# ELU feature map of the keys: exp straight from the copied keys with a fused min-add, and the next tile's layer norm emitted two groups earlier

## The reference, cut to what matters

```python
xn = layernorm(x)                                   # over 1024 channels
# attention part ("ripple"), 8 heads of 128 channels, S = 4096
q, k, v = split(xn @ Wqkv, 3)
tele = softmax(q . k[pos - offset] / sqrt(128)) @ v[pos - offset]   # offsets 0, 1, 2, 4, ..., 4096
conv = causal depthwise convolution of v, 7 taps
fq, fk = elu(q) + 1, elu(k) + 1
low  = fq @ (fk^T v) / (fq . sum(fk) + 1e-6)
attn = xn + (tele + conv + low) @ Wo
# ffn part
xr, xk = mu_r*xn + (1-mu_r)*shift(xn), mu_k*xn + (1-mu_k)*shift(xn)
ffn = sigmoid(xr @ Wr^T) * (relu(xk @ Wk^T)^2 @ Wv^T)
y = x + attn + ffn
```

## Time and profile before

| | us |
|---|---|
| median of 2 runs | 2516.59 |
| the two runs | 2481.43 and 2551.75 |
| the profiled execution, device time | 2494.07 |
| its span, slowest core (core 0) | 2492.4 |
| spans of the 8 cores | 2428.7 to 2492.4 |
| busy on core 0: PE / DVE / ACT / POOL | 1494.7 / 1427.4 / 687.4 / 117.9 |

### The profile page before, as it was taken

One profiled execution on the slowest core, in us unless ns is written; L12 is line 12 of the kernel. 1 busy time (PEld: TensorE's weight loads), 2 busy tenths in 40 slices (PEclk: granted clock), 3 DMA queues, 4 the chain that ended last, 5 costly groups with the idle time before them and its releaser, 6 DMA issues.

```text
span 2492.4 us, 32693 instructions; the slowest of 8 cores (2428.7 to 2492.4 us)
## 1 busy us (share of the span) xinstructions
PE 1494.7 (60%) x10400; PEld 826.0 (33%) x10400; DVE 1427.4 (57%) x2064; ACT 687.4 (28%) x960; POOL 117.9 (5%) x137
## 2 busy tenths in 40 slices
PE   0078766796668765777695336455464836365474
PEld 0033323233233332433343214233251716244261
DVE  0355764745648456485475683838374654837375
ACT  0033231322322313223141213233241514133141
POOL 0001010010010100101010000000000000000000
PEclk9998877777877778877696567677686968677786
DMA  9610402203113022030222604041311204040300
GB/s 150 107 43 26 137 33 68 87 16 111 59 34 110 26 85 85 15 130 26 60 77 57 163 9 122 14 118 19 106 31 57 81 0 128 9 119 18 110 19 34
DMA packets 75230, 168.08 MB, mean 67 GB/s; under 512 B 38080, under 2 KB 38208, under 8 KB 69952
## 3 DMA queue, kind: packets, MB, share of 16 engines
q1 hardware_dynamic: 59632, 100.98, 14.0%
q0 software_dynamic: 15440, 65.02, 9.7%
HBM read 113.55 MB, written 67.11 MB: 72 GB/s over the span
## 4 chain that ended last, share of the span: by engine, by line
PE 40%; DVE 28%; DMA 13%; issue 10%; ACT 7%; DVEq 1%; SPq 0%; POOL 0%; ACTq 0%; POOLq 0%
DVE s_zb L1018 8%; PE PS L465 6%; PE PS L602 5%; PE PS L545 5%; PE PS L573 5%; DVE s_cv L280 4%; PE PS L894 3%; PE PS L1051 2%; PE PS L632 2%; PE PS L943 2%; PE PS L898 2%; PE PS L1054 2%; DMA s_vr<-vt_sp 2%; PE PS L946 2%; DMA s_p<-p_sp 2%
## 5 line engine op out<-in xcount | busy, mean ns | idle before, releaser
L465 PE MATMUL PS<-s_xnfm,s_wq 128*128 128x512 bf16 x1536 | 387.7, 418 | 65.7 <-ACT s_qk L488 62.0
L280 DVE SCALAR_TENSOR_TENSOR s_cv<-s_vh,s_cw,s_cv 128x512 bf16<-128x512 bf16 x384 | 315.0, 820 | 44.6 <-DVE s_cv L280 3.2
L914 DVE RECIPROCAL s_rr<-PS 128x512 f32<-128x512 f32 x64 | 214.9, 3358 | 125.4 <-PE PS L898 125.2
L961 ACT ACTIVATE s_er<-PS,s_con 128x768 bf16<-128x768 f32 (+5 forms) x256 | 226.3, 887 | 162.2 <-PE PS L946 162.0
L465 PEld LDWEIGHTS PS<-s_xnfm,s_wq 128*128 128x128 bf16 x1536 | 159.5, 105 | 290.7 <-issue 182.8
L943 PE MATMUL PS<-s_q,s_kr 128*128 128x128 bf16 x1288 | 185.0, 229 | 114.0 <-DMA s_q<-q_sp 96.3
L1018 DVE RECIPROCAL s_zb<-s_zb 128x1024 f32<-128x1024 f32 x32 | 209.6, 6551 | 36.7 <-ACT s_zb L1013 36.7
L946 PE MATMUL PS<-s_id,s_mlog 128*128 128x128 bf16 x1288 | 186.2, 230 | 0.0
L943 PEld LDWEIGHTS PS<-s_q,s_kr 128*128 128x128 bf16 x1288 | 132.2, 103 | 120.5 <-issue 117.9
L1024 PE MATMUL PS<-s_fq,s_kvb 128*128 128x512 bf16 x32 | 18.7, 585 | 245.7 <-DVE s_h L1035 214.4
L894 PE MATMUL PS<-s_er,s_vr 128*128 128x128 bf16 x1288 | 118.9, 225 | 75.3 <-ACT s_er L961 45.8
(11 more groups left out here) (101 smaller groups left out, 1860.8 us busy)
## 6 DMA issues: line engine op xcount, KB each, us to landing
s_xa<-x SPq DMA_DIRECT2D x32, 512.0 KB, 4.4
s_xb<-x SPq DMA_DIRECT2D x32, 512.0 KB, 4.2
p_sp<-s_p POOLq DMA_DIRECT2D x32, 512.0 KB, 4.6
s_p<-p_sp SPq DMA_DIRECT2D x32, 512.0 KB, 10.2
y<-s_p SPq DMA_DIRECT2D x32, 512.0 KB, 4.2
q_sp<-s_qk POOLq DMA_DIRECT2D x8, 1024.0 KB, 4.1
k_sp<-s_qk POOLq DMA_DIRECT2D x8, 1024.0 KB, 4.2
vt_sp<-s_vt POOLq DMA_DIRECT2D x8, 1024.0 KB, 8.6
```

What stands on the lines that cost most here:

```text
L280: cinc(e.scalar_tensor_tensor(s1_cv[:, ch, :], src, s_cw[:, ch, j:j + 1], s1_cv[:, ch, :], ALU.mult, ALU.add))
L465: last = e.matmul(bank(bsel, 0, 512), s1_wq[:, kc, 128 * m:128 * (m + 1)], s1_xnfm[:, kc, 1:513], start=(kc == 0), stop=(kc == 7), skip_gr ...
L914: cinc(e.reciprocal(s2_rr[:, 512 * half:512 * half + 512], PS[:, 512 * (6 + half): 512 * (6 + half) + 512]))
L961: return e.activation(s2_er[:, eslot, 0:128 * n], src, AF.Exp, bias=s_con[:, 0:1], scale=s_con[:, 1:2])
```

## The change

Three edits in the QKV part of sweep 1:

1. The DVE minimum in front of the exponential goes. ACT takes Exp of the copied keys themselves, so its wait is for its own copy and no longer for DVE. The clamp comes afterwards: DVE computes max(k, 0) as before and then min(exp(k), 1) + max(k, 0) in one `scalar_tensor_tensor` where there was a `tensor_tensor` add. Since exp(min(k,0)) = min(exp(k),1), the result is the same function.
2. The four square roots are emitted behind the copy of m=4 where they stood behind m=6.
3. The normalisation of the next tile is emitted behind the feature map of m=9 where it stood behind m=11.

```diff
-            if m == 6 and st + 1 < NST and st + 1 < nst_lim:
+            if m == 4 and st + 1 < NST and st + 1 < nst_lim:
                 nstds = emit_ln_sqrt(st + 1, nvars)
@@
                 ch = m - 8
                 wts = [("act", qkv_evac[(st, m)])]
-                if ch >= 2:
-                    wts.append(("act", fkexp[ch - 2]))
-                W("vector", (lambda ch: lambda e: e.tensor_scalar(
-                    s1_rg[:, 4 + ch % 2, :], s1_qk[:, ch, :], 0.0, None, ALU.min))(ch),
-                    waits=wts, inc="dve")
-                fkmin[ch] = pl.val["dve"]
-                wts = [("dve", fkmin[ch])]
                 if ch == 0 and st > 0:
                     wts.append(("pe", trans_pe[st - 1]))
                 W("scalar", (lambda ch: lambda e: e.activation(
-                    s1_fk[:, ch, :], s1_rg[:, 4 + ch % 2, :], AF.Exp))(ch),
+                    s1_fk[:, ch, :], s1_qk[:, ch, :], AF.Exp))(ch),
                     waits=wts, inc="act")
                 fkexp[ch] = pl.val["act"]
 
                 def fka_fn(e, ch=ch):
                     cinc(e.tensor_scalar(s1_rg[:, 6 + ch % 2, :], s1_qk[:, ch, :], 0.0, None, ALU.max))
                     cwt(e)
-                    return e.tensor_tensor(s1_fk[:, ch, :], s1_fk[:, ch, :], s1_rg[:, 6 + ch % 2, :], ALU.add)
+                    return e.scalar_tensor_tensor(s1_fk[:, ch, :], s1_fk[:, ch, :], 1.0,
+                                                  s1_rg[:, 6 + ch % 2, :], ALU.min, ALU.add)
@@
-                if m == 11 and st + 1 < NST and st + 1 < nst_lim:
+                if m == 9 and st + 1 < NST and st + 1 < nst_lim:
                     emit_ln_norm(st + 1, nstds)
```

## The result

| | before | after |
|---|---|---|
| median, us | 2474.13 (10 runs, 2457.46 to 2551.75) | 2370.84 (11 runs, 2346.93 to 2443.78) |
| ratio | 1 | 0.9566, 95% interval 0.9519 to 0.9613 |

The changed kernel is faster by 4.3%, 107 us of 2474 by the ratio, with an interval of 96 to 119 us. The ratio leaves out executions in which one die ran at a lower clock; the medians and ranges are over all. Of the runs of before, two had been shown ahead of the prediction; with eight more the median is 42 us lower than it was.

A forecast was written before the change was run, and what follows sets the result against it. Each sweep 1 tile was taken as a serial loop of DVE, feature-map and PE pieces, 154.6 us. Savings of 94.8 (tiles 1 to 6), 9.7 and 3 make 107 us, giving 2387 or 2409, middle 2398; range 2352 to 2457.

The forecast's parts named there:

- The three pieces: A sweep 1 tile is one serial loop: DVE 60.2, feature map 26.4, PE 68.0 us; only the middle one changes.
- The k chain: ACT's key copies and Exps, 1.21 us a channel, let the next tile's transposes start 15.8 us earlier in tiles 1 to 6.
- Tile 0: First tile of sweep 1: k copy stays at 166.80, eighth Exp starts at 177.3 instead of 186.92, saving 9.7 us.
- tile 7: Tile without a next layer norm: saves the 1.75 us stall inside R and about 1.5 us of V, together 3.
- the slack before V: DVE's idle 3.15 us before V's multiply: used up but not overdrawn, as the convolution ends near R's start + 32.5.
- The gap in the q groups: PE waits for copies queued behind the square roots on ACT, losing some 4 to 5 us of q groups.
- half clock: Rival in the k phase: PE stays at half clock for seven groups, a tile saves 6.5 us, time 2453; chance 0.07.
- its base of 2505 us: Starting time behind the forecast 2398, the middle of 2387 (from the execution's 2494) and 2409 (from the two-run median).

The follow-up runs named there:

- the denser kernels: Changed kernel with R's matmuls right after the token shift, ratio 0.9359; plus convolution on head 4 behind V's products, 0.9258; or v and fk transposes between K and V groups, 0.8951.
- the last one above: Kernel with R's matmuls right after the token shift, plus transposes of v and fk between the groups of K and V; ratio 0.8951, 2225 us.

## Why the prediction was right

- *The three pieces.* Right: in tile 3 the first and the last are 60.2 and 67.9 us (60.4 and 68.0 before), and the middle one went from 26.3 to 10.4.
- *The k chain.* Counted as the prediction counts, from the start of the last copy of the token shift, the first k copy was put at T - 6.5 and came at T - 6.6, the first Exp at T - 4.5 and came there, the first copy of the transposes at T + 4.5 and came at T + 4.4, R at T + 10.6 and came there. The gap of the Exp behind ACT's own copy is 0.10 to 0.13 us, taken as 0.11 from a DVE row. That this gap, read on one engine, held on another was luck that the rows allowed, not something they showed.
- *The second edit* was priced at 1.2 us that are hidden; the runs show 1.0, hidden. *The third* was said to cover itself. It moves R by 2 us a tile and the period by 1.5; without it the six tiles would have saved some 9 us less.
- *Tile 0* saved 10.3 us in the median of the cores (R at T + 24.5 for T + 34.8), against 9.7; *tile 7* brought its add 1.8 to 5.2 us closer to T, median 3.7, against 3.
- *DVE.* The fused op was taken at 746 ns and takes 692 (group view, below), so the feature maps end at T + 12.7 as the prediction counts, for T + 13.9. The claim that the slack before V would be used up was too strong. In tile 3 of core 5 DVE again idles 3.15 us there, and R's 16.16 us for 15.18 helped; over tiles 1 to 6 of all cores the least idle time is 0.6 us and the median 1.5, where before it was 3.1 and 4.1. Nothing hung on it.

```profile
L510 DVE SCALAR_TENSOR_TENSOR s_fk<-s_fk,s_rg 128x512 bf16<-128x512 bf16 x64 | 44.3, 692 | 6.9 <-DVE s_rg L508 0.2
```

- *The clock.* The gap in the q groups came as worked out, 4.79 us. The granted clock was 1.00 in the groups before it and 0.52 in the first 8 of the 32 matmuls behind it, that is the level of 1.2 GHz, and 0.99 after; the 32 took 8.81 us for 7.07. The rule of the Trainium skill ("TensorE: Matmul & The Clock Gate", Part 1) that an idle PE slows down agrees with that. The rival "half clock" had seven groups at half clock; it was one, and these groups are wanted late enough. R, K and V of a tile ran at 0.96 or, in single tiles, at 0.77, as before.

The windows view of core 5 after, tiles 3 and 5, beside the earlier trace rows:

```profile
600.00:645.00 45.00, 42.87 (x193) 0.96 0.04 13
...
880.00:936.00 56.00, 53.72 (x200) 0.77 0.03 10
```

- *The time.* The saving was put at 107 us and is 107 by the ratio. The traces add up to the same: the medians give 15.5 us in each of tiles 1 to 6 (R 16.0 earlier, the piece from the first add to T 0.5 longer), 10.3 in tile 0 and 3.7 in tile 7, and the rest of the program, sweep 2 included, takes 1133.3 us after the last tile's first add, for 1132.5. The time, 2398 against 2371, is off by its base of 2505 us, 31 above the median of before: the two runs shown lay 7 us and 78 above the median of ten. The profiled execution was long too, because on core 0 R, K and V of tiles 2, 4 and 6 took until the next add 80 us where the others took 68, some 35 us in all.

## What to carry to other kernels

When one engine hands each slice to another and gets it back, look at what else stands in the two queues: here a 0.29 us minimum that stood behind DVE's token shift kept ACT idle for 7.6 us, and with ACT the copies that feed PE. An algebraic turn that puts the clamp behind the exponential moves the dependency to the side where nobody waits. And read a wait by who is queued in front of the releaser: the profile named DVE's add, but getting DVE's normalisation done 3.9 us earlier moved R by nothing before the handover was gone, and by 2 us a tile after.

## What the runs showed that I had not expected

The granted clock of 0.77 over R, K and V, which costs 11 us in a tile, fell in single tiles on two neighbouring cores at a time, in every profiled execution that has it. In the execution profiled after, in the window of tile 2, it is cores 2 and 3 (windows view, PE: length, busy, PEclk), while cores 0 and 1 of the same die are at 0.93:

```profile
core 1: us, PE busy (x), PEclk, DMA share, GB/s
459.00:515.00 56.00, 47.91 (x246) 0.93 0.07 27
...
core 2: us, PE busy (x), PEclk, DMA share, GB/s
459.00:515.00 56.00, 52.22 (x202) 0.79 0.03 10
...
core 3: us, PE busy (x), PEclk, DMA share, GB/s
459.00:515.00 56.00, 53.79 (x195) 0.77 0.03 10
```

The Trainium skill ("TensorE: Matmul & The Clock Gate", Part 1) says of the peak-current limiter that it takes a whole die; if this is that limiter, these traces do not agree. Mean clocks of executions that were not profiled look different: in one of the changed kernel, 2432.07 us, all of cores 4 to 7 had 0.75 to 0.76 and all of cores 0 to 3 had 0.81. Whether that is the same effect on both pairs of a die was not found out, nor why one pair and not another. In the profiled executions the denser kernels did not get more of it: the last one above has it on cores 2 and 3 alone, in two tiles. It is part of what decides the slowest core of an execution, and so of the scatter of the ratios: the longer of the two executions behind the 0.973 of the kernel with only the feature map changed has such a pair by its spans and mean clocks, cores 4 and 5. It was not profiled, so that this is the whole of its difference is not shown.
